# Products of two channels side by side in two column tiles of TensorE: the triangle stage of a four-layer network on Trainium2

## What is computed

```python
zn = _sparse_norm(z, alpha_in, beta_in)
a = jax.nn.sigmoid(_lin(zn, W_ga, b_ga)) * _lin(zn, W_la, b_la)
b = jax.nn.sigmoid(_lin(zn, W_gb, b_gb)) * _lin(zn, W_lb, b_lb)
k = jnp.einsum('bitc,bjtc->bijc', a, b)
kn = _sparse_norm(k, alpha_o, beta_o)
return jax.nn.sigmoid(_lin(zn, W_go, b_go)) * _lin(kn, W_lo, b_lo)
```

## Time and profile before

| | |
|---|---|
| time, median of three runs | 10102.23 us (10084.09, 10102.23, 10106.75) |
| profiled execution: span from first to last instruction | 10099.2 us |
| a time of the profiled execution beside its span | none is recorded; the median of the runs is 3.0 us above the span |
| TensorE busy, records | 8239.5 us (82% of the span), 38652 |
| this stage | from 9453.8 us to about 9702 us of the span |
| mean granted TensorE clock | 0.915 of 2.4 GHz |

### The profile page before, as it was taken

One profiled execution on the slowest core, in us unless ns is written; L12 is line 12 of the kernel. 1 busy time (PEld: TensorE's weight loads), 2 busy tenths in 40 slices (PEclk: granted clock), 3 DMA queues, 4 the chain that ended last, 5 costly groups with the idle time before them and its releaser, 6 DMA issues. The chain is left out here.

```text
span 10099.2 us, 123081 instructions
## 1 busy us (share of the span) xinstructions
PE 8239.5 (82%) x38652; PEld 5866.9 (58%) x38652; DVE 6910.6 (68%) x9163; ACT 4383.7 (43%) x8385; POOL 4337.9 (43%) x3061
## 2 busy tenths in 40 slices
PE   5878777877787887589999999958758999896667
PEld 3444344434443444379999999957545555554456
DVE  7999799979997999745555555533256666553446
ACT  4666566656664666422222222222314444453331
POOL 5999599959995999521111111100010000010001
PEclk8999999999998999899999999979858999998678
DMA  4555355535553555300000000031311000103000
GB/s 148 166 164 164 107 166 166 164 107 165 164 166 96 176 164 163 107 17 15 15 12 15 10 15 12 10 108 34 132 43 34 20 15 20 29 1 136 21 22 19
DMA packets 333429, 834.34 MB, mean 83 GB/s; under 512 B 35940, under 2 KB 111976, under 8 KB 318798
## 3 DMA queue, kind: packets, MB, share of 16 engines
q1 hardware_dynamic: 332822, 826.64, 27.0%
HBM read 758.85 MB, written 39.08 MB: 79 GB/s over the span
## 5 line engine op out<-in xcount | busy, mean ns | idle before, releaser
L888 POOL TENSOR_TENSOR ss_work<-ss_dtu,ss_ringb 128x768 f32<-128x768 f32 x1536 | 2760.3, 1823 | 251.0 <-POOLq L59 247.6
L750 PE MATMUL ss_ps<-ss_work,ss_ident 128*128 128x512 f32 (+1 forms) x6144 | 2312.3, 523 | 605.7 <-POOL ss_work L898 579.1
L750 PEld LDWEIGHTS ss_ps<-ss_work,ss_ident 128*128 128x128 f32 x6144 | 1205.1, 204 | 1492.8 <-issue 1292.2
L872 DVE TENSOR_TENSOR_SCAN ss_work<-ss_ps,ss_last,ss_work 128x768 f32<-128x768 f32 x1024 | 1813.6, 1809 | 64.2 <-ACT ss_ps L803 52.3
L803 ACT ACTIVATE ss_ps<-ss_dt,ss_a_neg 128x768 f32<-128x768 f32 x1536 | 1374.6, 895 | 287.4 <-DVE ss_work L872 270.2
L857 DVE TENSOR_TENSOR ss_work<-ss_work,ss_ps 128x1152 f32<-128x1152 f32 x768 | 1024.4, 1334 | 1.2 <-ACT ss_ps L811 1.2
L2464 DVE TENSOR_REDUCE at_top<-at_ps 128x1 f32<-128x384 f32 x1512 | 729.0, 548 | 407.1 <-PE at_ps L2382 407.1
L1386 ACT ACTIVATE stu_XT<-cv_ps 128x384 fp32r<-128x384 f32 x768 | 377.3, 491 | 1408.2 <-DVE cv_ps L1441 1096.5
L2445 ACT ACTIVATE at_probs<-at_ps 128x768 f32<-128x768 f32 x864 | 653.6, 808 | 664.2 <-PE at_ps L2401 663.3
L872 DVE TENSOR_TENSOR_SCAN ss_work<-ss_ps,ss_work 128x768 f32<-128x768 f32 x512 | 879.3, 1746 | 52.0 <-issue 18.0
L1292 POOL TENSOR_TENSOR cv_near<-cv_raw,cv_one 128x768 fp32r<-128x768 f32 (+1 forms) x32 | 46.9, 1467 | 1754.0 <-PE cv_ps L1316 1745.6
(11 more groups left out here) (565 smaller groups left out, 14296.8 us busy)
## 6 DMA issues: line engine op xcount, KB each, us to landing
ss_ringb<-scan_rows SPq DMA_DIRECT2D x768, 384.0 KB, 3.6
ss_ringc<-scan_rows SPq DMA_DIRECT2D x768, 384.0 KB, 3.9
c_w<-in_l_ffn_w SPq DMA_DIRECT2D x52, 1024.0 KB, 13.3
at_packs<-at_high SPq DMA_DIRECT2D x64, 288.0 KB, 5.5
c_w_last<-in_l_ffn_w SPq DMA_DIRECT2D x12, 1024.0 KB, 12.5
cv_raw<-in_l_ffn_phi_odd SPq DMA_DIRECT2D x16, 576.5 KB, 3.5
cv_raw<-in_l_ffn_phi_even SPq DMA_DIRECT2D x16, 576.0 KB, 4.1
at_packs<-at_qk SPq DMA_DIRECT2D x32, 288.0 KB, 5.5
```

The lines of the kernel that those rows point to most:

```text
L750: return pe.matmul(acc[:, d * WIN + a:d * WIN + e], ident[:, :], weighed[:, t % DEEP, d, a:e], start=n == 0 and e - a == 512, stop=n == NS ...
L872: dve.tensor_tensor_scan(hid[:, t % DEEP, d, ::step], decay[d][:, ::step], drive[:, t % DEEP, d, ::step], start, ALU.mult, ALU.add).then_i ...
L888: pool.tensor_tensor(drive[:, t % DEEP, d, :], dtu[:, t // NST % 2, d, :], ringb[:, t % RING, :], ALU.mult).then_inc(s["driven"], 1)
```

## The change

The 128 channels are treated as two halves of 64. Each step now makes the products of channels c and c + 64: the first with its output on partitions 0 to 47, the second on partitions 64 to 111 of the same PSUM bank. A group still is 8 channels of each half, so there are 8 groups with 16 products each. A copy out of PSUM takes 112 partitions with 384 elements each. The rows 48 to 63 between the halves are cleared once (VectorE, with a semaphore `blank` for which TensorE waits at the start). `kimg` becomes [112, 48, 64] and is stored in two transfers, one for each half of the channels; in DRAM each then writes runs of 64 floats (256 bytes) with a step of 512 bytes.

```diff
-    GROUPS_C = C // 8
+    CHANNELS = C // 2
+    GROUPS_C = CHANNELS // 8
...
-        ab, kimg = sb("ab", [W, 2, H, C]), sb("kimg", [H, H, C])
+        ab, kimg = sb("ab", [W, 2, H, C]), sb("kimg", [BUSY, H, CHANNELS])
...
+        def made_of(n):
+            return ps[0:BUSY, 4 + n % 4, 0:8 * H].rearrange("i (c j) -> i j c", c=8)
...
                     if b and n == 0:
-                        act.wait_ge(s[f"stored{b - 1}"], 16)
-                    act.activation(kimg[:, :, 8 * n:8 * n + 8], ps[0:H, 4 + n % 4, 0:8 * H].rearrange("i (c j) -> i j c", c=8), ACT.Copy).then_inc(s["kept_act"], 1)
+                        act.wait_ge(s[f"stored{b - 1}"], 32)
+                    act.activation(kimg[:, :, 8 * n:8 * n + 8], made_of(n), ACT.Copy).then_inc(s["kept_act"], 1)
...
-                    dve.tensor_copy(kimg[:, :, 8 * n:8 * n + 8], ps[0:H, 4 + n % 4, 0:8 * H].rearrange("i (c j) -> i j c", c=8)).then_inc(s["kept_dve"], 1)
-
+                    dve.tensor_copy(kimg[:, :, 8 * n:8 * n + 8], made_of(n)).then_inc(s["kept_dve"], 1)
+
+                dve.memset(ps[32:GAP, 4:8, :], 0.0).then_inc(s["blank"], 1)
...
                     for c in range(8):
-                        ins = pe.matmul(ps[0:H, 4 + n % 4, c * H:(c + 1) * H], ab[0:W, 0, :, 8 * n + c], ab[0:W, 1, :, 8 * n + c], start=True, stop=True)
+                        for half in range(2):
+                            channel, at = CHANNELS * half + 8 * n + c, GAP * half
+                            ins = pe.matmul(ps[at:at + H, 4 + n % 4, c * H:(c + 1) * H], ab[0:W, 0, :, channel], ab[0:W, 1, :, channel], start=True, stop=True, skip_group_check=True)
                     ins.then_inc(s["made"], 1)
 
                 pe.wait_ge(s["cleared"], 1)
+                pe.wait_ge(s["blank"], 1)
...
-                    sp.dma_start(k_dram[b * S:(b + 1) * S, :].rearrange("(i j) c -> i (j c)", i=H), kimg[:, :, :].rearrange("i j c -> i (j c)")).then_inc(s[f"stored{b}"], 16)
-                    sp.wait_ge(s[f"stored{b}"], 16)
+                    for half in range(2):
+                        sp.dma_start(k_dram[b * S:(b + 1) * S, CHANNELS * half:CHANNELS * (half + 1)].rearrange("(i j) c -> i j c", i=H), kimg[GAP * half:GAP * half + H, :, :]).then_inc(s[f"stored{b}"], 16)
+                    sp.wait_ge(s[f"stored{b}"], 32)
```

More of the change, by code:

```diff
@@ L2618, in triangle_products @@
         zimg, gates = sb("zimg", [P, H, GAP]), sb("gates", [P, 4, 2, C])
-        ab, kimg = sb("ab", [W, 2, H, C]), sb("kimg", [H, H, C])
+        ab, kimg = sb("ab", [W, 2, H, C]), sb("kimg", [BUSY, H, CHANNELS])
         ps = ctx.enter_context(nc.psum_tensor("tp_ps", [P, 8, 512], F32))
-        s = Signals(nc, "tp", "cleared staged projected gated multiplied made kept_act kept_dve stored0 stored1 stored2 stored3 loaded")
+        s = Signals(nc, "tp", "cleared blank staged projected gated multiplied made kept_act kept_dve stored0 stored1 stored2 stored3 loaded")
         flat = zimg[:, :, :].rearrange("p h w -> p (h w)")
@@ L2673, in keep @@
                     if b and n == 1:
-                        dve.wait_ge(s[f"stored{b - 1}"], 16)
-                    dve.tensor_copy(kimg[:, :, 8 * n:8 * n + 8], ps[0:H, 4 + n % 4, 0:8 * H].rearrange("i (c j) -> i j c", c=8)).then_inc(s["kept_dve"], 1)
+                        dve.wait_ge(s[f"stored{b - 1}"], 32)
+                    dve.tensor_copy(kimg[:, :, 8 * n:8 * n + 8], made_of(n)).then_inc(s["kept_dve"], 1)
+                dve.memset(ps[32:GAP, 4:8, :], 0.0).then_inc(s["blank"], 1)
                 for b in range(B):
```

## The result

The changed kernel takes 10069.69 us (median of 9 runs, 10065.19 to 10083.12) against 10101.94 us for the kernel before, run beside it (9 runs, 10084.09 to 10106.75). The ratio is 0.9972, with a 95% interval from 0.9963 to 0.9982 (18 to 37 us): faster by 0.28%, or 28 us. The two medians are 32 us apart. The forecast of 10052 was too low by 18 us, though its range holds the time.

What follows compares the result with a forecast made beforehand. It took TensorE's product stream, paced by stepped operand reading, as the bound. Products -53.6 and store +3.1 gave -50.5 against the span of 10099.2, so 10048.7, plus 3.0 made 10051.7 us; range 10038 to 10100.

Steps and rivals of the forecast that it cites:

- likeliest case: Products: full overlap of the two tiles' records, 50% chance, kernel at 10038 to 10062 us.
- The bound: Product phases, 4 x 27.6 = 110 us: TensorE's product stream binds, paced by stepped operand reading, not clock or issue.
- The products' term: Products: 128 rounds of two records at 110 ns, 14.1 us a batch in place of 27.5, saving 53.6 us in all.
- The rival with 25%, readings partly shared: Products: the two tiles' loads and matmuls hinder each other, 165 ns a round, -22.5 us with the store, 10080; chance 25%.
- The rule weighed against the change: Products: column tiles share rows, so a round's two loads go one after the other; saving 28 us in place of 53.6.
- The copies: Copies out of PSUM: 32 in place of 64, each still 0.48 or 0.55 us, off the path; 0 saved.
- The store: Store of kimg in 256-byte runs: only the last is in the open, +3.1 us, bounds -3.2 and +7.1.
- The blank: Clearing at the stage's start: some 1.8 us, hidden behind the copy into zimg; at worst 0.3 us.
- The clock: Projection behind each product phase: two slow pairs cost 2.1 us a batch today; taken as 0, bound -6.3 us.
- from span to time: Whole kernel: the median of the runs lies 3.0 us above the profiled span, so 10048.7 becomes 10051.7 us.

Runs made afterwards that it cites:

- the other order: Changed kernel with the second half's channels taken four further on within each group of 8, 16 bytes away from the first's: 10038.80 us, ratio 0.9945 to before.
- without alternation: Changed kernel, but each group does its 8 products of the first tile, then its 8 of the second: 10075.97 us, ratio 0.9976 to before.

## Why the prediction was right in its direction and wrong in its likeliest case

**The bound** was read rightly. What the product stream lost (27.4 to 21.9 us, four times: 21.9 us) is nearly all that the stage lost (22.6). That neither clock nor issue sets the pace, but the reading of stepped operands, was right too: padding alone moved it, at an unchanged count of instructions, and with rows 528 bytes apart a record takes 44 to 46 ns at either clock.

**The products' term** is the step that failed. The prediction took 110 ns for a round, by the unit-step tiles of the earlier trace rows, and 53.6 us of gain; a round took 170 ns and the gain was 21.9. The rival with 25%, readings partly shared (165 ns, -22.5 us in all), comes closest, and its evidence was in the rows: loads of 168 ns alone and 211 in company. That its time came out so near is luck. It priced 192 reads against a common limit of 0.83 ns each; with the same 192 reads a round took 91 ns once they were spread. What the prediction didn't see is where they meet: elements 512 bytes apart and channels 256 bytes apart all fall into one sixteenth of the memory. With the two tiles' readers in different parts the round is 109 ns (shown by the other order), spread over all parts 91. The range held the measured time because it reached up into this rival; the likeliest case alone, 10038 to 10062, did not.

**The rule weighed against the change** stands in the Trainium skill, TensorE: Matmul & The Clock Gate, Part 3: a load overlaps with running matmuls only when the row group differs. As the prediction read it, it would keep two 80-ns loads apart, 160 ns a round. The 91 ns with rows 528 bytes apart show that it doesn't hold for these tiles either. The rule of the Trainium skill, Advanced Engine Details and Errata, SBUF Cachelines, is that a line of 16 bytes wants at least two hits. The trace agrees: spread over all parts, a round of two tiles with stepped operands still takes 91 ns, while with unit step it takes 45 ns at the high clock.

**The copies** cost nothing, as forecast, but ScalarE's copy into `zimg` did not stay as it was. In the second batch it ended so late that the copies of PSUM banks behind it came late, and TensorE stood idle for one of them (0.18 us): that batch took 22.5 us against 21.6 to 21.9 for the others.

```profile
9533.33 12.18 ACT L2641 ACTIVATE tp_zimg<-tr_zt 128x2304 f32<-128x2304 f32 x1
...
9545.88 11.34 PE L2705 MATMUL tp_ps<-tp_ab 48*48 48x48 f32 x128 [0.18 <-ACT tp_kimg L2653]
```

The prediction had ScalarE as idle cover and didn't ask whether its reading would be disturbed.

**The store** was put at +3.1 us and is +0.5 (9.24 - 8.78, and 9.26 in the kernel before with this store alone). The price of a 512-byte run under a load from DRAM was no guide to a 256-byte run stored to it; the true value lies well inside the bounds of -3.2 and +7.1. The store beside the projection is covered, as forecast. The load behind it took 0.2 us less, so that from the last product to the end of the stage there are 17.7 us in place of 17.4.

**The blank** is hidden but for 0.08 us: it takes 1.765 us, as priced.

**The clock** fell to 0.50 in each product phase as before, but it came back at another place in the projections. Behind the first products the second gate followed the first after 1.30 us, where the earlier trace rows have 2.13:

```profile
9507.76 0.38 ACT L2647 ACTIVATE tp_gates<-tp_ps 112x256 f32<-112x256 f32 x1 [4.58 <-PE tp_ps L2696]
9509.06 0.38 ACT L2647 ACTIVATE tp_gates<-tp_ps 112x256 f32<-112x256 f32 x1 [0.92 <-DVE tp_ab L2673]
```

From the last product of a batch to the first of the next, the three projections took 29.4, 30.7 and 30.1 us against 30.1, 30.4 and 30.5 before: 0.8 us less in all. The 0 that was taken for the clock is close; the bound of -6.3 is far.

By the prediction's terms, then: -21.9 + 0.5 + 0.1 = -21.3 against -22.6 in the stage; the projections' 0.8 is the larger part of what is missing. The medians differ by 32 us, and their ratio's interval of 18 to 37 us holds the stage's 22.6. Between the two profiles 5.4 us lie outside the stage (2.1 ahead of it and 3.3 behind), where both programs are the same; the rest is within the spread of the runs, and no run here tells it apart. One more term was off: the prediction added 3.0 us from span to time, where the profiled execution of the changed kernel took 10073.03 us with a span of 10071.2.

## What to carry to other kernels

When TensorE reads with a step, look at the step's remainder modulo 256 bytes together with the work's shape: with a remainder of 0 all readers meet in one sixteenth of the memory. Of the stage, the tiles alone took 22.6 us here and the padding alone 19.0, but both together 62.6: once the padding kept the readers apart, the tiles were worth 43.6. In this case the sign was that records last longer in company than alone, in the engine itself and in a neighbour that only passes by. Compare them at one clock, since a lower clock makes them longer too. When rows of the same trace are taken as the price of a new operation, ask in which property they differ; here it was the step, and it decided.

## What the runs showed of the hardware that was not expected

- TensorE's stepped reading slowed another engine's copy in SBUF: ScalarE's from 2.1 to as much as 12.2 us with four readers in one part, but hardly with two (2.15 us without alternation, 2.21 with the other order) and not with rows 528 bytes apart (2.11).
- Neighbouring runs of instructions on different column tiles overlapped though the program didn't interleave them: 21.7 us a batch without alternation against 27.4 in one tile.
- Stepped writes of VectorE got slower when they were spread: 0.418 us with unit step, 0.593 with a step of 192 bytes, 0.685 with 208. Why isn't settled.
